# Rows of experts 1 to 7 turned by quarter moves and VectorE block transposes instead of TensorE transposes

## What is computed

```python
x = x + _L0_attn_ref(_layernorm(x, axis=-1), ...)          # recurrence: sigmoid gate, associative scan
...
dispatch, combine = _gating_top2(logits, C)                # C = 256 slots for each expert and group of 1024 tokens
expert_inputs = jnp.einsum('GSEC,GSM->EGCM', dispatch, x)
layer_w0 = jnp.einsum('EGCM,EMH->EGCH', expert_inputs, w0_kernel)      # M = 256, H = 1368
layer_w1 = jnp.einsum('EGCM,EMH->EGCH', expert_inputs, w1_kernel)
hidden = jax.nn.gelu(layer_w0, approximate=True) * layer_w1
expert_outputs = jnp.einsum('EGCH,EHM->EGCM', hidden, wo_kernel)
out = jnp.einsum('EGCM,GSEC->GSM', expert_outputs, combine)
```

## Time and profile before

| | us |
|---|---|
| median of 3 runs | 1680.05 (1678.08 to 1680.42) |
| profiled execution, its own time | 1687.82 |
| its span, first to last instruction | 1686.1 |
| TensorE busy | 1656.6 (98%) |
| VectorE busy | 866.2 (51%) |
| ScalarE busy | 724.1 (43%) |

### The profile page before, as it was taken

How to read it: one execution, slowest core, us unless ns; L and a number is a source line. 1 busy time by engine, 2 the same in 40 slices (tenths; PEclk the granted TensorE clock), 3 DMA queues, 4 the chain that set the end, 5 groups by cost and what they waited for, 6 DMA issues and landing times.

```text
span 1686.1 us, 22842 instructions
## 1 busy us (share of the span) xinstructions
PE 1656.6 (98%) x8738; PEld 1433.7 (85%) x8738; DVE 866.2 (51%) x1827; ACT 724.1 (43%) x1325; POOL 507.3 (30%) x433
## 2 busy tenths in 40 slices
PE   8999998999999999999999999999999999999998
PEld 6888887888888888888888888888888888888887
DVE  7998754345444553446444644455445544464442
ACT  5776544335433443335333533344334433353332
POOL 2156566562222222222222221222222222222211
PEclk9999999999999999999999999999999999999999
DMA  6553121035111421133111511151114211241111
GB/s 166 160 159 116 52 79 53 4 53 125 26 26 26 104 48 26 26 77 76 23 19 23 123 22 21 26 122 30 26 26 101 52 26 26 61 88 19 23 11 15
DMA packets 124980, 96.21 MB, mean 57 GB/s; under 512 B 27144, under 2 KB 120776, under 8 KB 124872
## 3 DMA queue, kind: packets, MB, share of 16 engines
q1 hardware_dynamic: 96200, 60.66, 13.2%
q0 software_dynamic: 28672, 34.10, 12.7%
HBM read 60.11 MB, written 34.61 MB: 56 GB/s over the span
## 4 chain that ended last, share of the span: by engine, by line
PE 90%; POOL 3%; DVE 2%; issue 2%; DMA 2%; another core or an unknown queue 0%; ACT 0%; POOLq 0%; SPq 0%; DVEq 0%; ACTq 0%
PE bank L1586 27%; PE bank L1599 27%; PE bank L1615 17%; PE bank L1617 9%; PE bank L1403 5%; POOL slots L599 2%; PE bank L1489 2%; PE bank L1456 1%; PE bank L1419 1%; PE bank L1610 1%; DMA slots<-records,sloti 1%; PE bank L1612 1%; PE bank L1444 1%; DVE y L947 0%
## 5 line engine op out<-in xcount | busy, mean ns | idle before, releaser
L1342 DVE TENSOR_TENSOR y<-bank,sig 128x512 f32<-128x512 f32 (+1 forms) x352 | 243.0, 690 | 466.0 <-PE bank L1599 437.7
L666 POOL DMA_INDIRECT out<-xring,slot_records x128 | 214.7, 1677 | 889.2 <-DVE xring L1322 824.5
L1615 PE MATMUL bank<-wo,hhi 128*128 128x512 f32 (+1 forms) x1276 | 447.4, 388 | 0.0
L851 ACT ACTIVATE hhi<-y 128x512 fp32r<-128x512 f32 (+1 forms) x349 | 220.4, 631 | 524.5 <-DVE y L1342 494.6
L1617 PE MATMUL bank<-wo,hlo 128*128 128x256 f32 (+1 forms) x1396 | 382.0, 274 | 0.0
L1345 DVE TENSOR_TENSOR hlo<-y,hhi 128x512 fp32r<-128x512 f32 (+1 forms) x349 | 241.5, 692 | 243.5 <-ACT hhi L851 236.5
L841 ACT ACTIVATE sig<-bank 128x512 f32<-128x512 f32 (+1 forms) x352 | 208.9, 594 | 284.2 <-PE bank L1586 269.4
L1615 PEld LDWEIGHTS bank<-wo,hhi 128*128 128x128 f32 (+1 forms) x1276 | 239.2, 187 | 43.7 <-DVE hlo L1345 0.2
L1617 PEld LDWEIGHTS bank<-wo,hlo 128*128 128x128 f32 (+1 forms) x1396 | 261.7, 187 | 7.1 <-issue 0.5
L1586 PE MATMUL bank<-xThi,whi 128*128 128x512 f32 x704 | 215.3, 387 | 2.7 <-ACT sig L841 1.2
L1599 PE MATMUL bank<-xThi,whi 128*128 128x512 f32 x704 | 212.7, 382 | 3.4 <-DVE y L1342 3.3
(11 more groups left out here) (134 smaller groups left out, 1566.8 us busy)
## 6 DMA issues: line engine op xcount, KB each, us to landing
stage<-in_L_ffn_w_kernel SPq DMA_DIRECT2D x160, 128.0 KB
stage<-in_L_ffn_wo_kernel SPq DMA_DIRECT2D x80, 128.0 KB
xring<-in_L_attn_x SPq DMA_DIRECT2D x16, 512.0 KB
out<-xring SPq DMA_DIRECT2D x16, 512.0 KB, 5.0
x_rows<-rows SPq DMA_DIRECT2D x16, 512.0 KB
slots<-records,sloti POOLq DMA_INDIRECT x128
rows<-x_rows,slot_records POOLq DMA_INDIRECT x128
out<-xring,slot_records POOLq DMA_INDIRECT x128, 3.8
```

The lines of the kernel that those rows point to most:

```text
L666: pool.indirect_dma_start(out_rows, bass.IndirectOffsetOnAxis(idx, 0), ysb[:, t % 2, j, :], None, compute_op=ALU.add).then_inc(added, 16)
L851: act.activation(h_high(e, t, hc)[0:n, :], hf[0:n, hc % 2, :], ACT.Copy).then_inc(h_hi, 1)
L1342: dve.tensor_tensor(hf[0:n, hc % 2, :], up_value(e, t, hc)[0:n, :], gel[0:n, hc % 2, :], ALU.mult).then_inc(mul_done, 1)
L1615: pe.matmul(lines(yb[j][:, :]), high, lines(wo[0:n, hc, :, :].rearrange("p s c -> p (s c)")), start=hc == 0, stop=end, skip_group_check=True)
```

## The change

For tiles 4 to 31 (experts 1 to 7) TensorE's `prepare` returns at once. In its place:

- **SyncE** issues `move_pieces(n)`, once the rows of tile n have landed: 16 transfers from `rows2` to `pieces`, each of 32 partitions x 4 x 64 values (32 KB, in runs of 256 bytes). Feature quarter c of slot quarter s goes to partitions 32c to 32c + 31. It stands in tile n - 2, behind the load of slot records, and in the fetch tile inside the row of weight loads, behind that of chunk 4.
- **VectorE** runs `turn_rows`, behind chunks 4 and 6 (`TURN`), one for each half k: a transpose of 32 x 32 blocks, 128 x 512 values, from `pieces` to `rowsT`. The block takes every second value, so partition p holds feature 2p + k.
- The up weights of experts 1 to 7 are loaded in the same order (feature 2p + k on partition p). Sizes and runs are unchanged.
- ScalarE and VectorE read `rowsT` (SBUF) in place of `tr` (PSUM) in `prepare`.
- The gather on GpSimd waits for the moves of the tile that held its half of `rows2`, not for TensorE.
- `pieces` lies in `rows[:, 0]` and `rowsT` in `xn`, which are used no longer by then.

```diff
+TURN = (4, 6)
...
+        rowsT = xn[:, :, :].rearrange("p j c -> p (j c)").rearrange("p (k t) -> p k t", k=KD)
+        pieces = rows[:, 0].rearrange("p j c -> p (j c)").rearrange("p (b j s c) -> p b j s c", b=2, j=FJ, s=NB)
...
+                order = "o (k p) h -> p (o k) h" if e == 0 else "o (p k) h -> p (o k) h"
...
+            def move_pieces(n):
+
+                p = n % 2
+                sync.wait_ge(rows_loaded[p], 16 * FJ * (n // 2 + 1))
+                if n >= FT + 2:
+                    sync.wait_ge(turned, KD * (n - 1 - FT))
+                for s in range(NB):
+                    for c in range(NB):
+                        sync.dma_start(pieces[32 * c:32 * (c + 1), p, :, s, :],
+                                       rows2[32 * s:32 * (s + 1), p, :, c * PW:(c + 1) * PW]).then_inc(
+                                           pieces_moved[p], 16)
...
                             weight_loads(sync, e + 1, hc)
+                            if hc == STAGES:
+                                move_pieces(FT * e + t + 2)
+                    elif FT <= FT * e + t + 2 < FT * E:
+                        move_pieces(FT * e + t + 2)
...
-                    pool.wait_ge(ft, KD * (n - 1))
+                    pool.wait_ge(ft, KD * min(n - 1, FT))
+                if n >= FT + 2:
+                    pool.wait_ge(pieces_moved[p], moved(n - 2))
...
+            def turn_rows(e, t, k):
+
+                n, p = FT * e + t, t % 2
+                dve.wait_ge(pieces_moved[p], moved(n))
+                blocks = pieces[:, p].rearrange("p j s c -> p (j s c)").rearrange("p (n i k) -> p k n i", i=32, k=KD)
+                dve.transpose(rowsT[:, k, :].rearrange("p (n i) -> p n i", i=32), blocks[:, k]).then_inc(turned, 1)
...
+                        if hc in TURN and FT <= FT * e + t + 1 < E * FT:
+                            turn_rows(*divmod(FT * e + t + 1, FT), TURN.index(hc))
...
             def prepare(e, t, k):
 
                 p = t % 2
+                if e > 0:
+                    return
```

More of the change, by code:

```diff
@@ L102, in build @@
     RING = 4
+    NB = P // 32
+    PW = D // NB
     GT1, GT2, EX1, TOK, SRC = range(5)
@@ L205, in build, with moved @@
         hf = y[:, 0]
+        rowsT = xn[:, :, :].rearrange("p j c -> p (j c)").rearrange("p (k t) -> p k t", k=KD)
+        pieces = rows[:, 0].rearrange("p j c -> p (j c)").rearrange("p (b j s c) -> p b j s c", b=2, j=FJ, s=NB)
+        def moved(n):
+            return 16 * NB * NB * ((n - FT) // 2 + 1)
         bank = [ctx.enter_context(nc.psum_tensor(f"bank{i}", [P, 512], F32)) for i in range(8)]
@@ L325, in build @@
         ft = sem("ft")
+        pieces_moved = [sem(f"pieces_moved{i}") for i in range(2)]
+        turned = sem("turned")
         fx_hi = sem("fx_hi")
@@ L380, in weight_loads @@
             for k, w in enumerate((w0_in, w1_in)):
-                src = w[bass.ds(e, 1), :, c].rearrange("o (k p) h -> p (o k) h", p=P)
+                order = "o (k p) h -> p (o k) h" if e == 0 else "o (p k) h -> p (o k) h"
+                src = w[bass.ds(e, 1), :, c].rearrange(order, p=P)
                 dst = stage[:, s, k * KD * P:(k + 1) * KD * P].rearrange("p (k h) -> p k h", k=KD)[:, :, 0:n]
@@ L756, in prepare @@
             def prepare(e, t, k):
-                act.wait_ge(ft, KD * FT * e + KD * t + k + 1)
-                act.activation(xThi[:, t % 2, k, :], tr[:, :], ACT.Copy).then_inc(fx_hi, 1)
+                if e == 0:
+                    act.wait_ge(ft, KD * t + k + 1)
+                    act.activation(xThi[:, t % 2, k, :], tr[:, :], ACT.Copy).then_inc(fx_hi, 1)
+                else:
+                    act.wait_ge(turned, KD * FT * (e - 1) + KD * t + k + 1)
+                    act.activation(xThi[:, t % 2, k, :], rowsT[:, k, :], ACT.Copy).then_inc(fx_hi, 1)
             def step(i):
@@ L1126, in prepare @@
                 dve.wait_ge(fx_hi, KD * FT * e + KD * t + k + 1)
-                dve.tensor_tensor(xTlo[:, p, k, :], tr[:, :], xThi[:, p, k, :].bitcast(F32),
-                                  ALU.subtract).then_inc(fx_lo, 1)
+                dve.tensor_tensor(xTlo[:, p, k, :], tr[:, :] if e == 0 else rowsT[:, k, :],
+                                  xThi[:, p, k, :].bitcast(F32), ALU.subtract).then_inc(fx_lo, 1)
+            def turn_rows(e, t, k):
[3 more added lines that the diff above has]
+                dve.transpose(rowsT[:, k, :].rearrange("p (n i) -> p n i", i=32), blocks[:, k]).then_inc(turned, 1)
             def first_weights(hc):
@@ L1482, in prepare @@
                 p = t % 2
+                if e > 0:
+                    return
                 if k == 0:
-                    pe.wait_ge(rows_loaded[p], 16 * FJ * (FT // 2 * e + t // 2 + 1))
+                    pe.wait_ge(rows_loaded[p], 16 * FJ * (t // 2 + 1))
                 else:
```

## The result

| | median, us | runs, us |
|---|---|---|
| before, beside it | 1679.07 | 1677.83 to 1680.42 |
| after | 1657.08 | 1654.96 to 1660.06 |
| predicted | 1654.0 | 1651 to 1663 |

The ratio is 0.987, with an interval of 0.9858 to 0.9883: 22.0 us less. The forecast was 26.0 less, so some 4 us are missing. A repeat gave 1657.77 us (1655.11 to 1659.54), ratio 0.987 (0.9855 to 0.9885).

A forecast was written before the change was run, and what follows sets the result against it. TensorE, busy 98% of the span, was taken to bound the kernel. Removed transposes gave 26.0 us and the added work nothing: 1680.05 - 26.0 = 1654.0 us for the median, range 1651 to 1663.

The forecast's parts named there:

- 56 x 0.465 = 26.0 us: TensorE, chunks 5 and 7 of tiles 4 to 31: 56 groups of four transposes removed, 0.465 us each.
- 0.69 us taken: VectorE: each of 56 added block transposes costs 0.69 us, 39 us in all, beside TensorE's work.
- The bound from the scan (1.27): VectorE, fetch tile: far-end price of a block transpose, 1.27 us against 1.25 of cover, about nothing lost.
- The moves in the fetch tiles of experts 1 to 6: SyncE's queue: 16 moves ahead of weight chunk 5's load, 5.5 to 8 us if issuing is the limit; 8 taken.
- in time by 1.4 us: Fetch tile of expert 1: weight chunk 5 lands at 588.0, ScalarE wants it at 589.4.
- the bound of 12.4 us: Fetch tiles: TensorE waits only when 16 moves take over 8 + 1.4 + 3.0 = 12.4 us, 0.78 each.
- I cost that at nothing: The other order of the weights, whose runs keep their size, and `prepare` reading SBUF: no cost.
- an estimate of 10.9 to 15.2 us: SyncE: 16 moves strictly one behind the other at the skill's prices; time then 1654 to 1674 us.
- The first moved tile: Tile 4: landing and moves, at most 3.5 + 8 us, fit before its turn 19.3 us into tile 3.
- weights a little late: Rival, fetch tiles: moves of 0.8 to 1.0 us each cost 3 to 25 us, 1657 to 1679 us; chance 0.08.
- small waits in every tile: Range term: unseen waits of half a microsecond a tile would give 1660 us.
- two rivals: VectorE's turn over 1.25 us, 1663 us, chance 0.07; and the smaller half of "weights a little late", chance 0.08.

The follow-up runs named there:

- order_only: The kernel before with only the new order of the up weights for experts 1 to 7: 1679.03 us, ratio 1.000.
- old_order: The changed kernel with the up weights of experts 1 to 7 loaded in the order of before: 1655.33 us, ratio 0.9854.
- no_moves: The changed kernel without the 448 moves, the turns kept: 1652.39 us, ratio 0.9837.
- added_only: The kernel before with moves and turns made but not used, TensorE's transposes and the old weight order kept: 1682.63 us, ratio 1.0017.

## Why the prediction was right, and where it was off

**TensorE: right.** 56 x 0.465 = 26.0 us. Measured 0.93 for each tile with two groups, and 26.3 us without moves. The stretches start to start, and not the sum of busy times, were the right source. By the Trainium skill's 390 ns for a 128 x 128 bf16 transpose on TensorE ("VectorE: DVE Perf Modes", The three transpose paths) it would have been an estimated 87 us. Here 26.3 / 224 is 0.117 us on the path, so for f32 transposes inside a stream of matmuls the runs don't agree with that price.

**VectorE: right.** 0.69 us taken, 0.705 measured, with every second value as the source (ns, least/median/most):
```profile
L1170 DVE STREAM_TRANSPOSE xn<-rows x56: 704/705/707, 389.5 to 1588.2; 128x512 f32<-128x512 f32 x56
```
The bound from the scan (1.27) was not needed. Taking the turns away gained nothing.

**The moves in the fetch tiles of experts 1 to 6: the mechanism right, each size somewhat short.** I took 0.50 us for an issue, by the weight loads. The row of after says 0.60 in the median:
```profile
L479 SPq DMA_DIRECT2D rows<-rows x448: 585/601/1749, 368.4 to 1546.0; - x150
```
With gaps, 16 take 10.4 to 11.6 us and not 8. The three issues of chunk 5 take 1.9 us and not 1.5, and ScalarE wants it 33.0 us into the tile, 0.5 sooner than reckoned. So "in time by 1.4 us" became a wait of ScalarE of 1.2 to 2.4 us, as in the fetch tile of expert 4:
```profile
1096.61 11.46 SPq L479 DMA_DIRECT2D rows<-rows  x16
```
```profile
1112.03 0.63 ACT L866 ACTIVATE whi<-stage 128x512 fp32r<-128x512 f32 x1 [2.38 <-DMA stage<-in_L_ffn_wo_kernel]
```
Most of that was taken up by the slack behind ScalarE. I had counted 3.0 us; the doubled moves show 12.07 - 9.68 = 2.4, and the bound of 12.4 us before TensorE waits becomes 11.7. 1.8 us in six tiles reached TensorE. "I cost that at nothing" for the other order of the weights was true alone (order_only) and not with moves in the queue, where the fetch tiles of old_order lose next to nothing. The issue was the limit, not the packets, as I had argued: a move lands 1.9 us after its issue while the next issue follows after 0.6, so several are under way. The Trainium skill's rule on small transfers ("DMA: Bandwidth & Descriptors", Bandwidth) had given an estimate of 10.9 to 15.2 us for 16 run one behind the other. The measured 10.4 to 11.6 lies about its lower end, but the moves didn't run one behind the other.

**The first moved tile: the step that failed.** "Landing and moves, at most 3.5 + 8 us, fit" asked only whether the turn of tile 4 gets its data in time. It does. But tile 4's rows are gathered only at the end of tile 2, so its moves are issued at the start of tile 3, and there the load of weight chunk 0 stands behind them, in the only expert change where the moves of a next tile and the first load fall together. The paragraph looked at who waits for the moves and not at what is queued behind them, which the fetch tiles' paragraph had done for chunk 5. It costs 4.0 us in the profiled execution, half as a stall, half as low clock. The rival "weights a little late" had the mechanism (1657 to 1679) at the wrong chunk and tile.

That chunk 0 is late has two parts. Tile 3 without moves (no_moves), then in added_only, then in old_order: of the issues of chunk 0 the first and the last, or the last alone, then its split.
```profile
378.34 1.29 SPq L396 DMA_DIRECT2D stage<-in_L_ffn_w_kernel  x2
379.67 0.60 SPq L397 DMA_DIRECT2D stage<-in_L_ffn_wo_kernel  x1
382.89 0.63 ACT L862 ACTIVATE whi<-stage 128x512 fp32r<-128x512 f32 x1 [2.01 <-DMA stage<-in_L_ffn_wo_kernel]
...
382.38 0.47 SPq L397 DMA_DIRECT2D stage<-in_L_ffn_wo_kernel  x1
388.15 0.63 ACT L862 ACTIVATE whi<-stage 128x512 fp32r<-128x512 f32 x1 [5.32 <-DMA stage<-in_L_ffn_wo_kernel]
...
382.96 0.47 SPq L397 DMA_DIRECT2D stage<-in_L_ffn_wo_kernel  x1
386.79 0.63 ACT L866 ACTIVATE whi<-stage 128x512 fp32r<-128x512 f32 x1 [3.35 <-DMA stage<-in_L_ffn_wo_kernel]
```

| tile 3 | first issue, us in | landing, us | wait of ScalarE | idle of TensorE | longer work |
|---|---|---|---|---|---|
| no_moves | 10.4 | 2.6 | 2.01 | 0 | 0 |
| after | 11.5 | 4.1 | 4.56 | 2.00 | 1.97 |
| added_only | 11.5 | 5.3 | 5.32 | 2.76 | 0.32 |
| old_order | 11.5 | 3.4 | 3.35 | 0.80 | 0.34 |

"Landing" is from the end of the chunk's last issue to the split that waits for it. From no_moves to after, whose weights have the same order, ScalarE waits 2.55 us longer: 1.1 for the later issue behind the moves, 1.4 for the landing. And TensorE is idle for the wait less 2.55 us, in all three runs with moves: that is the slack behind ScalarE here.

**The chances.** The result, 1657.08, is within the range, and faster by 1.3%. It lies at the low end of that rival and not at the forecast. That it is in the range is in part luck: the range went up to 1660 for small waits in every tile and to 1663 for two rivals, and no term of it stood for tile 3.

**Open.** The losses of tile 3 (4.0 us in after, 3.1 in added_only, 1.1 in old_order) differ although the moves take 10.5 us and the load is issued 11.5 us into the tile in all three. The table says where: in the landing and in the clock. Why the landing differs no run separates. With moves the gather of tile 5 is issued just ahead of chunk 0 (379.16 and 379.57 in after), without them just behind (387.64 and 387.18 in before), and the last moves are still under way; either may be the cause.

## What to carry to other kernels

Read what removed work is worth from stretches with and without it, start to start, at the engine that bounds the kernel; that term held to 0.3 us here. For added transfers, write out for each place the queue in which they are issued and list what stands behind them, the first round as well as the steady one: 16 moves of 32 KB held this queue for 10.4 to 11.6 us, and a load behind them was both issued later and landed later. Where a stall of TensorE of a few us is possible, allow for a low clock behind it: here up to 2 us for a stall of 2.0 and up to 2.4 for one of 9.7, but only 0.3 for one of 2.76.

## What the runs showed of the hardware

- The access order of a load from DRAM changes how long its issue holds SyncE: 0.467 us in the median before, 0.600 with "(p k)", for the load of `wo` too, whose own form didn't change and which is issued right behind the two changed ones. The row in after:
```profile
L397 SPq DMA_DIRECT2D stage<-in_L_ffn_wo_kernel x88: 337/599/1455, 10.5 to 1472.1; - x88
```
- A move of 32 KB within SBUF, in runs of 256 bytes, holds the queue for 0.60 us in the median and lands in 1.9 (longest 3.3).
- A block transpose of 128x512 on VectorE with a source of every second value takes 705 ns, 12 ns more than the subtraction of the same size (693).
- After a stall of 2.00 us the mean granted clock was 0.50 for 3.4 us; in added_only TensorE was idle for longer in tile 3 (47.95 - 45.19 = 2.76 us) with a mean clock of 1.00. A stall alone doesn't always bring the low clock, and the runs don't tell what decides it.
